# Gathering the z_in rows of the 55 resident node groups during the edge moves instead of after them (a graph-network layer, one core)

## What is computed

```python
in_deg = jnp.minimum(jax.ops.segment_sum(ones, dst, num_segments=num_nodes), MAX_IN_DEGREE - 1)
out_deg = jnp.minimum(jax.ops.segment_sum(ones, src, num_segments=num_nodes), MAX_OUT_DEGREE - 1)
edge_proj = edge_attr @ W_sum + b_sum
sum3d = jax.ops.segment_sum(edge_proj, src, num_segments=num_nodes)
cent_term = jax.nn.sigmoid(centralities @ W_cent + b_cent)
vor_term = jax.nn.sigmoid(voronoi_values @ W_vor + b_vor)
return x + z_in[in_deg] + z_out[out_deg] + cent_term + vor_term + sum3d
```

## Time and profile before

| | |
|---|---|
| median of 3 runs | 3068.58 us (3068.52 to 3073.89) |
| the profiled execution | 3061.41 us, span 3059.6 us |
| busy | DVE 1777.5 us, POOL 1857.0, PE 1690.0, PE weight loads 1297.1, ACT 771.3 |
| mean granted TensorE clock | 0.713 |
| DMA | 465.45 MB in the span, mean 152 GB/s |

### The profile page before, as it was taken

The page is one execution under the profiler, slowest core; times in us unless marked ns, Lnnn a source line. Parts: engine busy times, 40 slices in busy tenths (PEclk is TensorE's granted clock), DMA queues, the critical chain, the costliest instruction groups (busy, mean ns, idle before and its releaser), DMA issues.

```text
span 3059.6 us, 41787 instructions
## 1 busy us (share of the span) xinstructions
PE 1690.0 (55%) x9095; PEld 1297.1 (42%) x9095; DVE 1777.5 (58%) x6055; ACT 771.3 (25%) x3973; POOL 1857.0 (61%) x1869
## 2 busy tenths in 40 slices
PE   4645545555555333555554555555555566667776
PEld 1234333444344222444444444444444455555655
DVE  6555456666666532555655665544444455558878
ACT  3322222333233331332332332222222222200111
POOL 5666666656555665555555565555656565567787
PEclk7656677666656555777767777777777677879888
DMA  4255333334444443555555555556556566679896
GB/s 126 86 147 159 103 105 109 107 110 132 117 131 123 138 127 111 150 159 147 165 145 156 161 169 148 167 168 169 165 165 173 148 189 186 187 180 235 209 238 174
DMA packets 499624, 465.45 MB, mean 152 GB/s; under 512 B 74023, under 2 KB 459181, under 8 KB 499372
## 3 DMA queue, kind: packets, MB, share of 16 engines
q1 hardware_dynamic: 417326, 313.53, 39.5%
q0 software_dynamic: 78752, 136.44, 14.1%
q10 hardware_dynamic: 3294, 12.80, 1.3%
HBM read 332.60 MB, written 129.73 MB: 151 GB/s over the span
## 4 chain that ended last, share of the span: by engine, by line
another core or an unknown queue 33%; DVE 22%; PE 16%; issue 13%; ACT 5%; DMA 4%; POOL 4%; DVEq 2%; SPq 0%; POOLq 0%; ACTq 0%
PE bank L994 8%; ACT junk L868 5%; DVE hot_n L670 4%; POOL sorted L513 3%; DVE hot_dh L605 3%; DVE acc L697 3%; DMA edge_ring<-in_L_gnn_z_out_dram,out_i 3%; DVE hot_dl L605 3%; PE bank L942 2%; PE bank L977 1%; DVE gate_normed L736 1%; PE bank L971 1%; DVE hot_t L605 1%; PE bank L978 1%
## 5 line engine op out<-in xcount | busy, mean ns | idle before, releaser
L513 POOL DMA_INDIRECT sorted<-edge_ring,pos_i x1660 | 1600.5, 964 | 1112.1 <-DVE pos_i L803 632.9
L994 PE MATMUL bank<-piece_ring,hot_n 128*125 128x129 f32 x5320 | 959.0, 336 | 328.7 <-DVE hot_n L670 248.9
L994 PEld LDWEIGHTS bank<-piece_ring,hot_n 128*125 128x125 f32 x5320 | 882.9, 240 | 460.6 <-DVE hot_n L670 300.3
L868 ACT ACTIVATE junk<-bank,mark_col 128x100 bf16<-128x100 f32 x1664 | 548.5, 341 | 1828.8 <-remote 1385.4
L697 DVE TENSOR_TENSOR acc<-bank,acc 125x129 f32 x1330 | 376.3, 283 | 701.0 <-remote 534.8
L670 DVE SCALAR_TENSOR_TENSOR hot_n<-bank,wkey,piece_ring 128x250 f32<-128x250 f32 x1330 | 621.5, 468 | 10.1 <-DMA piece_ring<-sorted 8.9
L977 PE MATMUL bank<-hot_w,after_b 128*128 128x400 bf16 x416 | 187.2, 450 | 629.2 <-ACT junk L868 472.8
L1019 PE MATMUL bank<-hot_dl,hot_dh 128*125 128x100 bf16 x1661 | 212.6, 280 | 273.7 <-DVE hot_dh L605 235.6
L868 ACT ACTIVATION_READ_ACCUMULATOR junk<-bank,mark_col 128x1 f32 x1664 | 337.0, 203 | 5.1 <-issue 5.1
L977 PEld LDWEIGHTS bank<-hot_w,after_b 128*128 128x128 bf16 x416 | 50.1, 120 | 673.0 <-ACT junk L868 502.0
L605 DVE TENSOR_TENSOR hot_dl<-dst_parts,bank 128x400 bf16<-128x400 bf16 x416 | 146.0, 351 | 317.8 <-remote 281.9
(11 more groups left out here) (107 smaller groups left out, 1205.2 us busy)
## 6 DMA issues: line engine op xcount, KB each, us to landing
piece_ring<-sorted SPq DMA_DIRECT2D x1330, 130.0 KB
edge_ring<-in_edge_attr_dram SPq DMA_DIRECT2D x332, 320.0 KB
sorted<-edge_ring,pos_i POOLq DMA_INDIRECT x1660
base<-in_x_dram SPq DMA_DIRECT2D x20, 560.0 KB
out_dram<-base ACTq DMA_DIRECT2D x19, 560.0 KB
out_dram<-base SPq DMA_DIRECT2D x9, 560.0 KB
base<-out_dram SPq DMA_DIRECT2D x9, 560.0 KB
edge_ring<-in_L_gnn_z_out_dram,out_i POOLq DMA_INDIRECT x100
```

The source lines that it names most:

```text
L513: g.indirect_dma_start(rows, bass.IndirectOffsetOnAxis(index, 0), edge_ring[:, slot, at, :], None).then_inc(s_scatter[slot], 16)
L868: last = a.activation(junk[:, t, :], part[:, t // 2, :, t % 2], ACT.Relu, bias=mark_col[:, :], accum_out=pos_f[:, q % 4, t:t + 1])
L994: last = t_.matmul(to, hot_n[:, n % HOT_SLOTS, k, :], piece_ring[:, n % PIECE_SLOTS, k, 0:SUM], start=(k == 0), stop=(k == ROW_GROUPS[s] - 1))
```

## The change

The z_in gathers of the 55 resident groups leave the tail. Each of them is now issued by POOL inside the quad loop, after the scatters of quads 290, 292, ... 398, into six places of `dst_parts` (free since the in-degrees were counted), and is added by DVE eight quads later, in the new side item `early`, at the end of the side work of quads 298, 300, ... 406. POOL waits before gather w (w of 6 and more) for add w-6; DVE waits before an add for its gather's landing. In the tail the 15-place ring now serves z_out alone, POOL starts with the 18 guest gathers, and the adds of resident z_in are gone. The places and semaphore counts of the guest ring go on from the early uses.

```diff
+EARLY_LEAD = 8
+EARLY_PLACES = 6
...
-        for line in ("hist", "node"):
+        if not todo["node"] and node_end == NQ:
+            node_end = q
+        for line in ("hist", "node", "early"):
             while q >= KEYS1 and todo[line]:
                 kind, b, part = todo[line][0][1]
+                if kind == "early" and (q < node_end + EARLY_LEAD or q % 2):
+                    break
+                if kind == "early":
+                    early_quad[b] = q
...
-    tail_adds = sorted([(4 + w * (ahead + 20) // ROW_SLOTS if w < ROW_SLOTS
-                         else ahead + BACK_LAG + (w - ROW_SLOTS) * (NW - BACK_LAG - 5) // GUESTS, "z_in", w) for w in range(NW)]
+    tail_adds = sorted([(ahead + BACK_LAG + (w - ROW_SLOTS) * (NW - BACK_LAG - 5) // GUESTS, "z_in", w) for w in range(ROW_SLOTS, NW)]
...
-            pool.wait_ge(s_in_deg, 1)
+                for w in [w for w in range(ROW_SLOTS) if early_quad[w] - EARLY_LEAD == q]:
+                    place = w % EARLY_PLACES
+                    if w == 0:
+                        pool.wait_ge(s_in_deg, 1)
+                    if w >= EARLY_PLACES:
+                        pool.wait_ge(s_early, w - EARLY_PLACES + 1)
+                    g.indirect_dma_start(z_places[1][place][0:NODE_P, :], None, z_in[:, :],
+                                         bass.IndirectOffsetOnAxis(deg_i[0:NODE_P, w:w + 1], 0)).then_inc(s_z_row[1][place], 16)
+            pool.wait_ge(s_early, ROW_SLOTS)
             wait_scattered(pool, NT)
...
+            def early(w):
+
+                place = w % EARLY_PLACES
+                dve.wait_ge(s_z_row[1][place], 16 * (w // EARLY_PLACES + 1))
+                dve.wait_ge(s_node, NW)
+                row = base[0:NODE_P, w, :]
+                v.tensor_tensor(row, z_places[1][place][0:NODE_P, :], row, ALU.add).then_inc(s_early, 1)
```

More of the change, by code:

```diff
@@ L66 @@
         "hist": (0.7, 1.0, 0.0), "stats": (0.62, 0.0, 0.0), "degrees": (2.0, 0.0, 0.0), "indegrees": (0.3, 0.0, 0.0),
-        "clear": (0.0, 0.0, 2.5), "node": (2.3, 0.0, 1.3), "piece2": (0.75, 0.66, 0.0)}
+        "clear": (0.0, 0.0, 2.5), "node": (2.3, 0.0, 1.3), "early": (0.45, 0.0, 0.0), "piece2": (0.75, 0.66, 0.0)}
 def gnn_kernel(nc, x, src, dst, edge, cent, vor, z_in, z_out, w_cent, b_cent, w_vor, b_vor, w_sum, b_sum,
@@ L139, in gnn_kernel @@
                      + [(0, ("node", j, (j > j0) + 2 * (j < j1))) for j in range(j0, j1 + 1)]],
-            "stats": [(0, ("stats", j, 0)) for j in range(NW)]}
+            "stats": [(0, ("stats", j, 0)) for j in range(NW)],
+            "early": [(0, ("early", w, 0)) for w in range(ROW_SLOTS)]}
+    node_end = NQ
+    early_quad = [NQ - 1] * ROW_SLOTS
     KEYS1 = quad0[1] + KEYS - SRC_KEYS
@@ L195, in gnn_kernel @@
                     x_quad[X_ORDER.index(b // X_WINDOWS - 1)] = q + REST_LOAD
-                if kind in ("node", "degrees"):
+                if kind in ("node", "degrees", "early"):
                     break
     assert not todo["totals"] and not todo["stats"]
-    after = [x[1] for kind in ("piece", "hist", "node") for x in todo[kind]]
+    after = [x[1] for kind in ("piece", "hist", "node", "early") for x in todo[kind]]
     side_ahead = [side[q] for q in range(PIECE_AHEAD, NQ)]
@@ L218, in gnn_kernel @@
     ring_of = {g: (ring, n, order_) for ring, order_ in enumerate((others, guests)) for n, g in enumerate(order_)}
+    early_uses = [len(range(i, ROW_SLOTS, EARLY_PLACES)) if i < EARLY_PLACES else 0 for i in range(max(GATHERS, GUEST_GATHERS))]
     store_start = list(range(0, SW - STORE_WINDOWS + 1, STORE_WINDOWS)) + [SW - 2, SW]
@@ L314, in gnn_kernel @@
         s_piece_in = [sem(f"s_piece_in{i}") for i in range(PIECE_SLOTS)]
+        s_early = sem("s_early")
         s_z_row = ([sem(f"s_z_row{i}") for i in range(GATHERS)], [sem(f"s_z_guest{i}") for i in range(GUEST_GATHERS)])
@@ L774, in add_to_row @@
                     dve.wait_ge(s_guest[(w - ROW_SLOTS) // X_WINDOWS], 64)
-                before = [added[kind_, w] for kind_ in ("z_in", "bias", "product", "z_out") if added[kind_, w] < added[kind, w]]
+                before = [at for kind_ in ("z_in", "bias", "product", "z_out") for at in [added.get((kind_, w), NQ)]
+                          if at < added[kind, w]]
                 if before:
@@ L787, in add_to_row @@
                     places = z_places[ring]
-                    dve.wait_ge(s_z_row[ring][n % len(places)], 16 * (n // len(places) + 1))
+                    landed = n // len(places) + 1 + (early_uses[n % len(places)] if ring == 1 else 0)
+                    dve.wait_ge(s_z_row[ring][n % len(places)], 16 * landed)
                     last = v.tensor_tensor(row, places[n % len(places)][0:NODE_P, :], row, ALU.add)
@@ L837, in _ @@
                         indegrees()
+                    elif what == "early":
+                        early(s)
                     elif what == "piece":
@@ L842, in _ @@
             dve.wait_ge(s_node, NW)
+            dve.wait_ge(s_early, ROW_SLOTS)
             for c in range(pieces[NS - 1] + Z_LAG):
```

## The result

The changed kernel takes **3111.6 us** (median of 4 runs, 3103.0 to 3113.5), the kernel before 3071.2 us in the runs beside it (4 runs, 3068.5 to 3077.3): a ratio of 1.0131, 95% interval 1.0112 to 1.0151. It is some 40 us slower; 18 us faster were forecast. The profiled execution has a span of 3109.8 us against 3059.6, at the same mean granted clock (0.712 and 0.713).

What follows compares the result with a forecast made beforehand. In the quads no engine was full and POOL and ACT/DVE waited for each other; DVE and DMA held the tail's first part. -22.8 (tail) + 0 (POOL) + 4.6 (adds) = -18.2 us from 3068.58 gave 3050.4 us, range 3010 to 3115.

Steps and rivals of the forecast that it cites:

- Added to the quads, POOL: Quads 290 to 398: 82.5 us of gathers hide in POOL's idle time; cost 0, up to 82.5 if not covered.
- slower rival: Quads 290 to 398: POOL's scatter string sets the pace, gathers lengthen it; 3133 us, 3092 at half price; chance 0.32 in all.
- The pause is there: Quads: argument against the slower rival, that POOL idles 3.0 to 3.5 us per two quads, twice a gather's need.
- Gathers in the tail run back to back with DVE and PE going on beside them: Tail: argument against the slower rival, that gathers there, 1.50 us from start to start, don't stop DVE and PE.
- the restart soon after POOL's last scatter: Quads: sign for the slower rival, ACT and DVE going on together about 1.7 us after POOL's last scatter ended.
- The tail: Tail's first part: 55 adds at 0.33 us (18.2) and a 4.6 us gather wait go; gain 22.8 us, bounds 5 to 30.
- The bound by bytes: Tail: if DMA holds it, removing 7.04 MB at 235 GB/s gains 30 us, the upper bound.
- DVE's adds: Quads: 55 adds at 0.33 us ahead of casts, 18.2 us, at most 9 on the path; cost taken 4.6 us.
- the second way of the slower rival: Quads: each add stands until a POOL scatter (0.96 us) is out, 53 us, so 3103 us; chance 0.02.
- Waits added: Quads: POOL's wait for add w-6 and DVE's for a gather issued eight quads earlier cost 0.
- The faster rival: Quads: a gather between scatters lets ACT and PE go on; at most 88 us, at half 3006 us; chance 0.14.

Runs made afterwards that it cites:

- e8: Changed kernel without the 55 adds, each early gather fetching 64 bytes per node instead of 1 KB: 3116.1 us on chip B.
- e1: Changed kernel without its 55 early gathers, only the early adds kept: 3077.2 us, 0.9891 of the kernel before on chip A.
- e3: Changed kernel without the adds, each early gather replaced by a POOL iota of 1300 columns: 3059.2 us on chip A.

## Why the prediction was wrong

**The step that failed** is "Added to the quads, POOL": "Cost taken: 0. Cover: the wait for `pos_i`". The price was 75.4 us, near the upper bound of 82.5 that stood beside it. The reasoning took POOL's idle time for slack. It is slack against POOL's computing: 68 us of iotas in it cost nothing. It is none against an indirect DMA: in most pairs the others come back only after POOL's string has ended, and a gather puts that moment off by up to its 1.5 us. That is the slower rival as it was written, "a gather in the string lengthens each pair of quads by its 1.50 us, and POOL's idle time, which follows their restart, stays": the pair went from 13.2 to 14.6 us (718.3 and 793.7 over 54.5), POOL's idle from 300.8 to 304.3 us (without the 0.30 us ahead of each instruction, from 3.1 to 2.9 us a pair). It gave 3133 us at full price, 3092 at half; 3111.6 came. The stated range of 3010 to 3115 held that number through the part of it that stood for this rival, not through the forecast's own 3038 to 3062.

**What misled.** Two sentences against that rival. "The pause is there" is the same mistake. "Gathers in the tail run back to back with DVE and PE going on beside them" is true and didn't carry over: the waits for remote in the tail of before are one, of 0.9 us, while in the quads a gather prolongs them. The sign that spoke for it, the restart soon after POOL's last scatter, was right for 43 of ACT's 51 long waits.

**The tail**: 22.8 us forecast, 35.6 measured, beyond the bound of 30. Pieces near 0.65 us and PE late next came as put (0.63 us, PE 60.9 of 64 us busy). But the term was built from DVE's 0.33 us per add, and those by themselves give nothing; the gathers' absence alone gives 20.7. The bound by bytes, 30 us, was nearer in size; that bytes are the cause isn't shown. The z_out gathers' 10.8 us weren't counted at all.

**DVE's adds**: 4.6 us forecast. Gathers without adds took 792.3 us (e8), with them 793.7, which shows no cost. On chip A the adds alone took 731.7 us, 11 to 15 more than the kernel before on the other chips; how much of that is the chip no run separates. L737, with two inputs in SBUF beside a scattering POOL, takes 416 ns, as L789 did in the earlier trace rows; the second way of the slower rival didn't occur. The prediction has POOL busy some 80% of the time beside the earlier trace rows; it was 257.9 of 348.6 us, 74%.

**Waits added**: 0 forecast. POOL waited 0.3 us, once, for an add, and DVE never for a gather. **First 290 quads**: no term, and none shown.

**The faster rival** was wrong of gathers and right of pauses: 21 us in the same quads from 55 iotas, 82 us from 156 (3062.8 - 2981.0).

The sum with measured terms: -35.6 + 75.4 - 1.5 = +38 us, where the medians differ by 40.4.

## What to carry to other kernels

An engine's idle time is slack only for work of a kind that doesn't prolong what the idle time follows: ask who ends it, and whether the new instruction puts that off. Before work is moved into a gap, try the gap with an instruction that only takes time; where that is free and the real one isn't, what it does is the price, and a deliberate gap may even gain. And time both on more than one chip: 156 pauses gained 2.8% on one kind, and 312 of about half the length cost 7.5% on the other, where the engine that pauses is the bound.

## What the runs showed of the hardware

- While POOL issued indirect DMAs with 0.3 us between them, ACT and DVE stood for something that the profile calls remote, on four chips of six. In the kernel before ACT went on within 2.5 us after a string's end in 43 of 51 long waits of quads 290 to 398. 55 iotas of 1.23 us or 55 plain DMAs of 0.58 us put into the string shortened the stretch by 21 and by 22 to 24 us, 55 indirect gathers of 1.23 us lengthened it by 75. In the pair of the earlier trace rows the add that DVE began at 2646.64 us didn't stand for PE's result, since PE had no matmul between 2641.80 (2640.31 + 1.49) and 2647.38. What is held up, and why it isn't in the tail, no run shows.

```profile
2640.31 1.49 PE L994 MATMUL bank<-piece_ring,hot_n 128*125 128x129 f32 x12
2647.38 2.08 PE L994 MATMUL bank<-piece_ring,hot_n 128*125 128x129 f32 x8 [5.58 <-DVE hot_n L670]
```

- Of the same kernel two kinds of chips made 3063 to 3111 us and 2471 us, with the same duration of a scatter (966 and 968 ns). On the faster kind no wait for remote shows, with and without pauses; whether it is the chip or how it is set up stays open.
- An indirect gather took POOL a mean of 1230 ns for rows of 1 KB and 1229 for rows of 64 bytes, a plain DMA of the same rows of 1 KB 575 ns.

Open as well: why pauses gain 1 us each in quads 185 to 289 and almost nothing before quad 185, and whether a pause behind a gather makes up for it on a chip of the first kind; that kernel ran on the other kind alone. The tail of e1 took 10 us longer than that of e3 on the same chip with the same instructions (325.6 and 315.5), unexplained.
